# A three-block decoder kernel: the position bias raises TensorE's signals by a drain behind each group

## The reference

```python
pos_emb = rpe[hops]                                  # hops: (256, 256) indices, rpe: (2017, 256)
pe = pos_emb.reshape(Sq, Sq, NH, DH)                 # NH = 8 heads of DH = 32
k_hop = jnp.einsum('bhvc,vmhc->bhvm', qh, pe)        # the position bias
qk = jnp.einsum('bhsd,bhtd->bhst', qh, k_scaled)
C = (qk + k_hop) * D
```

## Time and profile before

| what | value |
|---|---|
| median of 3 runs | 1079.46 us (1077.34 to 1087.96) |
| the profiled execution | 1084.22 us, of which the span of its instructions is 1082.4 us |
| mean granted TensorE clock | 0.789 |
| TensorE busy over the span | 867.1 us (80%), 5868 MATMUL records |
| GpSimd busy over the span | 449.4 us (42%), of it 257 gathers: 252.8 us |
| line 861, transposes | 514 of the position bias, 104.3 us |
| line 887, products | 1028 records, 178.3 us |

### The profile page before, as it was taken

One profiled execution on the slowest core, in us unless ns is written; L12 is line 12 of the kernel. 1 busy time (PEld: TensorE's weight loads), 2 busy tenths in 40 slices (PEclk: granted clock), 3 DMA queues, 4 the chain that ended last, 5 costly groups with the idle time before them and its releaser, 6 DMA issues. The chain is left out here.

```text
span 1082.4 us, 17254 instructions
## 1 busy us (share of the span) xinstructions
PE 867.1 (80%) x5868; PEld 786.5 (73%) x5869; DVE 416.2 (38%) x910; ACT 352.5 (33%) x886; POOL 449.4 (42%) x453
## 2 busy tenths in 40 slices
PE   4887889657778777679989879556099999999995
PEld 2666677547767767579878868454099999999994
DVE  2355564542323221123347787542223222322220
ACT  1333233151313121223354544231043444344431
POOL 4555552046767666640054544105513323332332
PEclk9989999957575667789955555555599999999998
DMA  7222221064333323220054330297512222222221
GB/s 229 71 85 85 69 80 38 11 210 117 88 88 89 97 88 93 88 69 1 11 180 122 112 98 30 67 378 255 179 29 39 35 35 39 37 32 39 39 31 20
DMA packets 70564, 94.77 MB, mean 88 GB/s; under 512 B 17672, under 2 KB 59088, under 8 KB 70512
## 3 DMA queue, kind: packets, MB, share of 16 engines
q0 software_dynamic: 19488, 43.16, 15.8%
q1 hardware_dynamic: 51024, 50.92, 15.5%
HBM read 76.97 MB, written 17.07 MB: 87 GB/s over the span
## 5 line engine op out<-in xcount | busy, mean ns | idle before, releaser
L257 POOL DMA_INDIRECT G<-in_rpe,hopi x257 | 252.8, 984 | 173.5 <-issue 58.0
L887 PE MATMUL ps<-U,PET 128*128 128x64 f32 (+3 forms) x768 | 138.9, 343 | 49.8 <-DVE PET L771 22.4
L887 PEld LDWEIGHTS ps<-U,PET 128*128 128x128 f32 x768 | 134.4, 263 | 57.9 <-ACT PET L917 25.9
L1602 PEld LDWEIGHTS ps<-G,QT 128*128 128x128 f32 x1248 | 147.7, 194 | 1.9
L1602 PE MATMUL ps<-G,QT 128*128 128x128 f32 x1248 | 147.8, 277 | 0.0
L1653 ACT ACTIVATE G<-ps,U 128x128 f32<-128x128 f32 x312 | 85.0, 384 | 184.3 <-PE ps L1602 184.3
L1611 PE MATMUL ps<-G 128*128 x624 | 141.2, 379 | 0.9 <-DVE G L1700 0.9
L1611 PEld LDWEIGHTS ps<-G 128*128 128x128 f32 x624 | 115.5, 190 | 15.4 <-issue 1.3
L917 ACT ACTIVATE PET<-ps 128x512 f32<-128x512 f32 (+1 forms) x65 | 38.4, 593 | 225.2 <-PE ps L861 160.2
L861 PE MATMUL ps<-cst,G 128*128 128x128 f32 x514 | 104.3, 338 | 3.8 <-issue 3.8
L771 DVE COPY PET<-ps 128x512 f32<-128x512 f32 x64 | 43.9, 689 | 162.7 <-PE ps L861 103.9
(11 more groups left out here) (219 smaller groups left out, 1231.5 us busy)
## 6 DMA issues: line engine op xcount, KB each, us to landing
G<-run_max SPq DMA_DIRECT2D x16, 768.0 KB, 5.3
U<-in_w SPq DMA_DIRECT2D x8, 1024.0 KB
G<-in_w SPq DMA_DIRECT2D x8, 1024.0 KB
slot_rows<-cst SPq DMA_DIRECT2D x1, 5167.5 KB
G<-slot_rows SPq DMA_DIRECT2D x39, 128.0 KB
G<-in_rpe,hopi POOLq DMA_INDIRECT x257
U<-in_ctx SPq DMA_DIRECT2D x8, 256.0 KB
out<-X SPq DMA_DIRECT2D x1, 2048.0 KB
```

What stands on the lines that cost most here:

```text
L257: pool.indirect_dma_start(out=dst, out_offset=None, in_=rpe_d, in_offset=bass.IndirectOffsetOnAxis(ap=hopi[:, n:n + 1], axis=0)) \
L887: mm = pe.matmul(o, pet[:, n % 2, j, :], rhs, start=True, stop=True, skip_group_check=True)
L1602: mm = pe.matmul(bank(1 + 2 * u + c // 4, 4, P)[:, c % 4], w1c[u][:, k, c * P:(c + 1) * P], hT[u][:, k, :], start=(k == 0), stop=(k == KC ...
```

## The change

Behind the last matmul of `turn(q)` and of `products(q)` stands a drain on TensorE, and the semaphore is raised by it. Transposes and products raise nothing any more. That is 129 drains for `turned` and 129 for `prod`, 258 in all. Who waits for which value is as before, and so is the order of all other instructions.

```diff
--- before.py
+++ after.py
@@ -858,8 +858,8 @@
                     for n in tiles(q):
                         src = rows_of(n)
                         for j in range(KC):
-                            mm = pe.transpose(o[:, n % 2, j, :], src[:, j * P:(j + 1) * P], ident)
-                    mm.then_inc(turned, 1)
+                            pe.transpose(o[:, n % 2, j, :], src[:, j * P:(j + 1) * P], ident)
+                    pe.drain().then_inc(turned, 1)
 
                 def products(q):
                     pe.wait_ge(pet_r[q % 2], q // 2 + 1)
@@ -884,8 +884,8 @@
                             else:
                                 o = mixed(g)[:, j, :, :, n % GRP]
                                 rhs = QA[:, k % 2, n % QP, j].rearrange("p t h b -> p t (h b)")
-                            mm = pe.matmul(o, pet[:, n % 2, j, :], rhs, start=True, stop=True, skip_group_check=True)
-                    mm.then_inc(prod, 1)
+                            pe.matmul(o, pet[:, n % 2, j, :], rhs, start=True, stop=True, skip_group_check=True)
+                    pe.drain().then_inc(prod, 1)
 
                 for g in range(2):
                     for c in range(2):
```

## The result

The changed kernel took 1147.9 us (median of 4 runs), the kernel before 1078.4 us beside it: 1.063 times as long, with a 95% interval of 1.055 to 1.071. The profiled execution of the changed kernel had a span of 1150.0 us against 1082.4, so there are 67.6 us to explain.

A forecast was written before the change was run, and what follows sets the result against it. The stage was taken to be bound by late arrival of TensorE's two signals while gathers run. Holes add 19 us without gathers and 32 with them: 1084.2 + 19 + 32 = 1135, or 1079.5 + 51 = 1130 us against the median; range 1040 to 1190.

The forecast's parts named there:

- What bounded the kernel: Stage of the change: TensorE's signals seen up to 10 us late while gathers run, 2.90 us a pair against 1.31 without.
- (c): Part with gathers, 87 pairs: signals as late as now, holes of 0.51 us a pair added, 27% hidden: +32 us.
- the faster rival: Part with gathers: the drain's signal is on time; 1000 to 1107 us by the clock; gain over 1%: chance 0.23.
- second condition: Part with gathers: a gain over 1% also needs the full clock for more than about 0.35 of that part.
- on time, never at the full clock: Part with gathers: signals on time at clock 0.5, 2.99 us a pair, +8 us; with +19 elsewhere, 1107 us.
- A drain has to know that those same matmuls are complete: TensorE, part with gathers: the delay hits matmuls long out of TensorE, and the drain must await their completion; argument for late signals.
- The hole: TensorE's stream, each group: lost overlap plus 0.06 us restart, 0.225 us at full clock, 0.27 at half.
- The clock in the part without gathers: Last 42 pairs: clock stays 1.0, holes cost +19 us; the rival, a fall to 0.5, gives +71 there, 1182 in all.
- The other stages: Outside the changed stage: lengths should stay the same within 2 us.

## Why the prediction was right, and where it was wrong

The time (1130 forecast, 1148 measured) and the side are right. The way there is right in part, and that the sum came near has luck in it: the forecast was +51 us, and of the 67.6 measured 9.5 lie in the first block, which the change doesn't touch, and about half of the rest has another cause than forecast.

**What bounded the kernel** was read rightly: the lateness of the signals made the part with gathers cost 2.90 us a pair. Where signals are on time the same code takes 235 us for the stage instead of 313.

**"(c) As late as now in the mean, with only the holes added"** is the step that failed. With the change most signals were on time: 251 of 258 drains ended 0.02 us behind the last matmul, and most copies started 0.06 us behind it. That was the condition of the faster rival. It did not become a gain because of its second condition, the clock: it was at 1.0 for a third of the part before and at 0.5 from 241 to 463 us after. The case "on time, never at the full clock", priced at +8 + 19 and 1107 us, is nearly what happened, and it had no chance of its own. (c) gave +32 us for the part with gathers and about +31 was measured (60.3 less the 29 of the part without), by another mechanism. That the two agree is luck.

**"A drain has to know that those same matmuls are complete"** carried (c), and it was held against the faster rival too. The records agree with it: each of the 258 drains ends at least 0.02 us behind the last matmul, and behind the 7 late ones TensorE stood for up to 1.87 us. It misled me because I read it as "as late as the matmul's signal in the kernel before", which came up to 9.8 us late, and 251 of the drains were not.

**The hole** was mis-sized: 0.225 us a group at the full clock and 0.27 at half were forecast; (2.01 - 1.31) / 2 = 0.35 and (3.29 - 2.45) / 2 = 0.42 were measured. The overlap lost was read rightly. What was missing was in the rows: a group that starts from standing is itself longer. The products behind a late copy last 1.97 us, those in the stream 1.81, and I took only the 0.06 us ahead of them for the restart. Behind a drain they last 1.96 and 1.97. In the part without gathers this makes 42 x 0.70 = 29 us instead of 19. At half clock it makes a pair 3.29 us instead of 2.99, 26 us over 87 pairs, and that is most of what "+8" lacked.

**The clock in the part without gathers** did not fall, as forecast: 1.00 with holes.

**The other stages** were to keep their length within 2 us. What follows did (2.2 us); the first block took 9.5 us more, for no reason in the change.

**What the timely signals were worth.** Where they were late, the change cost 60 us in the stage, and where they were not, 121. So ending most of the lateness was worth about half of what the drains cost. That is an inference from two pairs of runs on different machines.

**What stays open.** None of the twelve experiments met late signals, so it was not shown what delays them. Whether the drains or only TensorE's slower pace (with it GpSimd waits 96.3 us for TensorE between gathers, and 36.8 before) brought most of them on time was not tested either. The changed kernel's first profile speaks for the pace: the drains stand in the queue throughout, and yet signals are late again where the clock comes up while gathers run, and only there. A drain alone did not put these 7 signals on time.

## What to carry to other kernels

Each drain in TensorE's stream cost the overlap of two groups and the weight load that had run ahead, 0.35 to 0.42 us, and it cost the same where it signalled nothing (1117.7 against 1114.1 us); the holes between narrow matmuls cost more by the clock than by themselves (85 of 120 us). Before pricing an edit that puts gaps into TensorE's stream, look at which clock its stage runs, and price both levels, with a chance for each. A stall that "remote" or idle listeners show may belong to the machine, as here (2.90 us a pair on one, 1.74 on another): run the kernel before somewhere else before curing it.

## What was not expected of the hardware

The same program took 1078 us on one machine and 992 to 995 on three others, and 78 of the 93 us between the two profiled spans (1082.4 and 989.3) lie in the stage with dense gathers, 12 in the first block, which has gathers as well. The signals of TensorE's matmuls were up to 9.8 us late there. Those of ScalarE and VectorE were not seen late (products that waited for a copy started 0.05 to 0.06 us behind it). With drains, 7 signals were still late there, by up to 1.66 us, all while gathers ran and within 13 us of a rise of the clock.

The clock of the drained stream was not the same with products of another width: 0.50 from 250 to 430 us with 64 columns, and 1.00 from 250 to 440 us where most had 128, at the same count of matmuls and drains. Widening them made the drained kernel 85 us faster although it doubles the columns of seven of eight of the narrow ones.
